# Two-layer graph convolution with scatter: final scatter moved last, dense work re-tiled in pairs of 1024 rows and spread over all stages

## The reference

```python
msg = x[src] @ W_msg + edge_attr @ W_edge
agg = segment_max(msg, dst)            # -inf -> 0 where a node has no edge
out = leaky_relu(agg + x @ W_root + b) # slope 0.01
```

## Time and profile before

| what | value |
|---|---|
| median of 3 runs | 1419.96 us (1419.81 to 1425.56) |
| profiled execution, span from first to last instruction | 1697.5 us (the page gives no other time of it) |
| DVE, POOL busy | 1044.2 us (62%), 1055.8 us (62%) |
| PE, ACT busy | 978.8 us (58%), 666.9 us (39%) |
| granted PE clock, mean | 0.746 |
| DMA | 245.87 MB, 145 GB/s over the span |

### The profile page before, as it was taken

The page is one execution under the profiler, slowest core; times in us unless marked ns, Lnnn a source line. Parts: engine busy times, 40 slices in busy tenths (PEclk is TensorE's granted clock), DMA queues, the critical chain, the costliest instruction groups (busy, mean ns, idle before and its releaser), DMA issues.

```text
span 1697.5 us, 21367 instructions
## 1 busy us (share of the span) xinstructions
PE 978.8 (58%) x3038; PEld 438.7 (26%) x3038; DVE 1044.2 (62%) x3881; ACT 666.9 (39%) x1717; POOL 1055.8 (62%) x1182
## 2 busy tenths in 40 slices
PE   3476866666666465687778778454343443334441
PEld 1233433233333232332322223222111111111210
DVE  2356666555555465679999999665544555445553
ACT  1345654444444354568888888400000000000000
POOL 5566656455545545617877767666667766677665
PEclk9678877778777777889999999755655655556555
DMA  6366756556555455755444444533333333233320
GB/s 172 93 183 207 240 178 181 174 175 194 175 177 184 146 179 171 220 177 185 157 153 154 152 146 154 164 111 106 104 95 94 107 99 104 79 102 99 107 74 21
DMA packets 142053, 245.87 MB, mean 145 GB/s; under 512 B 31470, under 2 KB 70120, under 8 KB 142022
## 3 DMA queue, kind: packets, MB, share of 16 engines
q1 hardware_dynamic: 103462, 161.26, 30.4%
q0 software_dynamic: 31360, 45.90, 11.5%
q10 hardware_dynamic: 7200, 38.40, 6.0%
HBM read 122.70 MB, written 125.07 MB: 146 GB/s over the span
## 4 chain that ended last, share of the span: by engine, by line
issue 34%; DVE 15%; PE 15%; another core or an unknown queue 15%; ACT 11%; POOL 4%; DMA 1%; DVEq 1%; ACTq 1%; POOLq 1%
ACT ob L686 5%; PE ps L529 5%; PE ps_r L529 4%; DVE stat L820 3%; PE ps_t L519 2%; POOL out L302 2%; PE ps_m L529 2%; DVE c1t L780 2%; DVE mv L831 2%; ACT c2t L647 2%; POOL g_src L295 2%; DVE c2t L780 2%; DVE stage L923 1%; DVE mx L790 1%
## 5 line engine op out<-in xcount | busy, mean ns | idle before, releaser
L686 ACT ACTIVATE ob<-ps_y,shift,rstd 128x96 f32<-128x96 f32 x784 | 273.7, 432 | 139.9 <-DVE shift L859 71.4
L820 DVE BATCH_NORM_STATS2 stat<-ps_y 128x6 f32<-128x96 f32 x784 | 147.0, 248 | 192.4 <-remote 141.1
L302 POOL DMA_INDIRECT agg_table<-stage,now_end x196 | 221.2, 1128 | 68.5 <-issue 68.2
L302 POOL DMA_INDIRECT out<-stage,now_end x196 | 200.4, 1022 | 60.0 <-issue 59.1
L295 POOL DMA_INDIRECT g_src<-in_x,now_gat x196 | 195.8, 999 | 63.0 <-issue 62.9
L295 POOL DMA_INDIRECT g_dst<-in_x,now_gat x196 | 195.2, 996 | 59.7 <-issue 59.1
L529 PE MATMUL ps<-xtb,wr 97*96 97x512 f32 x392 | 224.1, 655 | 11.0 <-ACT c1t L647 2.9
L295 POOL DMA_INDIRECT g_src<-agg_table,now_gat x196 | 196.8, 1004 | 52.9 <-issue 52.6
L529 PE MATMUL ps<-c1t,wr 97*96 97x512 f32 x392 | 212.4, 625 | 11.5 <-issue 10.3
L519 PE MATMUL ps_t<-ident,g_src 128*96 128x128 f32 x392 | 90.2, 374 | 209.9 <-DMA g_src<-agg_table,now_gat 176.7
L655 ACT ACTIVATE std<-mv,epsc 128x4 f32<-128x4 f32 x245 | 74.6, 305 | 296.5 <-issue 185.5
(11 more groups left out here) (54 smaller groups left out, 1494.3 us busy)
## 6 DMA issues: line engine op xcount, KB each, us to landing
xtb<-in_xt SPq DMA_DIRECT2D x196, 192.0 KB
agg_table<-zero ACTq DMA_DIRECT2D x50, 750.0 KB
out<-ob SPq DMA_DIRECT2D x195, 192.0 KB
mask<-mask_row SPq DMA_DIRECT2D x98, 192.0 KB
xd_keep<-g_dst SPq DMA_DIRECT2D x49, 192.0 KB
root_keep<-rt SPq DMA_DIRECT2D x49, 192.0 KB
c1d_keep<-c1d SPq DMA_DIRECT2D x49, 192.0 KB
rt<-root_keep SPq DMA_DIRECT2D x49, 192.0 KB
```

The source lines that it names most:

```text
L302: nc.gpsimd.indirect_dma_start(out=rows, out_offset=bass.IndirectOffsetOnAxis(ap=now_end[:, e.slot(R), r:r + 1], axis=0), in_=stage[:, e.s ...
L686: last = nc.scalar.activation(ob[:, d.slot(R), row(r)], ps_y[k][:, row(r)], ACT.Identity, bias=shift[:, k, r:r + 1], scale=rstd[:, k, r:r ...
L820: last = V.bn_stats(stat[:, k, r, :], rows(r))
```

## The change

All 49-chunk loops are written out (no hardware loops). POOL's program becomes four sequences. The number of indirect DMAs stays 980:

- A: 49 x 4 gathers of `x[src]`, and 7 chunks' gathers of `x[dst]` (28) among them.
- S: 49 x 4 table scatters, each chunk waiting only for the parts of the table that its rows fall in to be cleared (a number that POOL reads from a tile into a register). Then 3 chunks' gathers of `x[dst]` (12).
- B: 49 x 4 table gathers and 39 chunks' gathers of `x[dst]` (156).
- O: 49 x 4 scatters into `out`, each chunk waiting for the dense stores of its part of `out` only.

Index copies on POOL, the bounds check of the scatters and the tile `stage` go; DMAs read the index tiles directly and scatter from `nat`. Rows that must not be written go to spare rows behind the N rows. Each gather waits for the one three chunks before it to have landed (`FLIGHT = 3`). Each tile of the source gathers has its own semaphore.

Dense work is tiled in 98 **pairs** of 1024 rows: 14 beside stage A, 35 beside S, 25 in B and 24 behind them. `x` is loaded a second time in row order. The second product takes c1 as the stationary operand, so its result has rows on the partitions and the transposes back go. Leaky sums are made as relu(0.99 u) (ACT, from PSUM) plus 0.01 u + x (DVE, written to PSUM). `bn_stats` takes two rows at a time with an interleaved pattern and yields mean and sum without `bn_aggr`. Of the 8 rows per partition that are normalized, DVE takes 2 and ACT 6 (in stage B ACT takes 8).

The clears are 49 DMAs of 768 KB, 25 issued in A and 24 in S. c1 at `dst` is recomputed in B from `x[dst]` and `nat`, so `c1d_keep` and `xd_keep` go, and PE does more in B.

```diff
-ZCOL = 1500
-NZ = N * D // (P * ZCOL)
+J = 8
+RS = 6
+RD = 10
+NA = 14
+NS = 35
+NM = 25
+VROWS = 2
+AHEAD = 4
+LAND = 8
+FLIGHT = 3
+ZA = 25
...
+STEPS_A = spread(NA, NCH, 0)
+STEPS_S = spread(NS, NCH, NA)
+STEPS_B = spread(NM, NCH, NA + NS)
+STEPS_Z = spread(ZA, NCH, 0)
+SEAM = 3
+EARLY = {t: (t - 8) // 5 for t in range(8, 8 + 5 * (RD - SEAM), 5)}
...
+            for c in range(NCH):
+                gather_src(x, c, c)
+                if c in EARLY:
+                    pool.wait_ge(s_prep, 12)
+                    gather_dst(EARLY[c], c)
+
+            for c in range(NCH):
+                last = (c + 1) * TPC - 1
+                pool.wait_ge(s_zeroed, nc.gpsimd.value_load(zone_i[P - 1:P, last:last + 1], min_val=1, max_val=NZ))
+                pool.sem_inc(s_open, 1)
+                pool.wait_ge(s_open, c + 1)
+                scatter(table, c, sc_t, a_nc)
+            pool.wait_ge(s_zeroed, NZ)
+            for c in range(RD - SEAM, RD):
+                gather_dst(c, NCH)
+            for k in range(LAND):
+                pool.wait_ge(sc_t[k], 16 * ((NT + LAND - 1 - k) // LAND))
+
+            for c in range(NCH):
+                gather_src(table[0:N, :], c, NCH + c)
+                if RD <= c + AHEAD < NCH:
+                    gather_dst(c + AHEAD, NCH + c)
+
+            for c in range(NCH):
+                last = (c + 1) * TPC - 1
+                pool.wait_ge(s_stored, nc.gpsimd.value_load(pair_i[P - 1:P, last:last + 1], min_val=1, max_val=NQ))
+                pool.sem_inc(s_under, 1)
+                pool.wait_ge(s_under, c + 1)
+                scatter(out, c, sc_o, e_done)
...
+                for j in range(HJ):
+                    last = nc.tensor.matmul(ps_z[:, h, row(j)], c1t[:, q % 2, cols(h * HJ + j)], wr2[:, :],
+                                            start=True, stop=True)
...
+                for r in range(TPC):
+                    nc.tensor.matmul(ps_n[:, row(r)], c1d[:, c % 2, cols(r)], wr2[:, :], start=True, stop=False)
+                    last = nc.tensor.matmul(ps_n[:, row(r)], mx2[:, c % 2, cols(r)], ident[0:D, 0:D],
+                                            start=False, stop=True)
...
+                    nc.tensor.matmul(ps_r[0:D, :], wr1[0:D, :], xd[:, c % 2, :], start=True, stop=False)
+                    for r in range(TPC):
+                        last = nc.tensor.matmul(ps_r[0:D, cols(r)], nat[:, c * TPC + r, :], ident[:, :],
+                                                start=False, stop=r == TPC - 1)
...
+                t = ps_z[:, h, 0:HJ * D]
+                V.scalar_tensor_tensor(out=t, in0=t, scalar=SLOPE, in1=xn[:, k, halfrow(h)],
+                                       op0=ALU.mult, op1=ALU.add).then_inc(d_u, 1)
...
+                for j in range(0, J, 2):
+                    last = V.bn_stats(stat[:, q % 2, j:j + 2, :].rearrange("p r s -> p (r s)"),
+                                      two_rows(yo[:, q % YR, j * D:(j + 2) * D]))
...
+                for j in range(on_vector(q)):
+                    t = yo[:, q % YR, row(j)]
+                    last = V.tensor_scalar(t, t, stat[:, q % 2, j, 1:2], rstd[:, q % 2, j:j + 1],
+                                           ALU.subtract, ALU.mult)
```

More of the change, by code:

```diff
@@ L46, with spread, gnn_kernel @@
 SLOPE = 0.01
-ZCOL = 1500
-NZ = N * D // (P * ZCOL)
[L49 to L113, removed]
+ZROWS = 2048
+ZCOL = ZROWS * D // P
+NZ = -(-N // ZROWS)
+ZTAIL = (N - (NZ - 1) * ZROWS) * D // P
+ZR = 4
+NA = 14
[6 more added lines that the diff above has]
+ZA = 25
+assert NZ == NCH and NQ == 2 * NCH and (N - (NQ - 1) * PN) % J == 0
+def spread(count, ticks, first):
+    return {t: range(first + t * count // ticks, first + (t + 1) * count // ticks) for t in range(ticks)}
+STEPS_A = spread(NA, NCH, 0)
+STEPS_S = spread(NS, NCH, NA)
+STEPS_B = spread(NM, NCH, NA + NS)
+LATE = NA + NS + NM
+STEPS_B[NCH] = range(LATE, LATE + 1)
+STEPS_B[NCH + 1] = range(LATE + 1, LATE + 2)
+STEPS_Z = spread(ZA, NCH, 0)
+STEPS_Y = {t: range(ZA + t, ZA + t + 1) for t in range(NZ - ZA)}
+SEAM = 3
+EARLY = {t: (t - 8) // 5 for t in range(8, 8 + 5 * (RD - SEAM), 5)}
+def gnn_kernel(nc, x, xt, src, dst, dst_next, dst_row, dst_prev, aside, eat,
                w1m, w1e, w1r, b1, w2m, w2e, w2r, b2, out):
@@ L637, in _ @@
+            for d in range(LATE + 1, NQ + 1):
+                for h in range(2):
+                    dense(range(d, d + 1), h)
         @block.scalar
@@ L728, in _ @@
-            clear(NZ - 1)
-            each_chunk(act, step_a)
-            maxima(LAST_CHUNK)
-            def step_s(q, s, last=False):
-                c = chunk(q, s)
-                act.wait_ge(a_nc, c.at + 1)
-                if c.reached(2):
-                    act.wait_ge(sc[c.slot(2)], 64 * c.turn(2))
-                copy(stage[:, c.slot(2), :], nat[:, ds(c.at * TPC * D, TPC * D)], s_stage)
-                for t in range(2):
-                    dense(block_s(q, s, t))
-            each_chunk(act, step_s)
@@ new lines, in dense_norm, with dense_head @@
+            def dense_norm(q):
+                if not real(q):
+                    return
+                act.wait_ge(d_shift, q + 1)
+                for j in range(on_vector(q), J):
+                    last = nc.scalar.activation(yo[:, q % YR, row(j)], yo[:, q % YR, row(j)], ACT.Identity,
+                                                bias=shift[:, q % 2, j:j + 1], scale=rstd[:, q % 2, j:j + 1])
+                last.then_inc(d_done_a, 1)
+            def dense_head(steps):
+                for d in steps:
+                    dense_std(d - 2)
+                    dense_r(d - 1, 0)
+                    dense_t1(d, 0)
@@ L758, in _ @@
+            for d in range(LATE + 2, NQ + 2):
+                dense_head(range(d, d + 1))
+                dense_tail(range(d, d + 1))
         @block.vector
```

1146 lines of the change are left out of this document (560 added, 586 removed).

## The result

The changed kernel takes **1245.9 us** (median of 4 runs, 1245.5 to 1246.9) against 1419.9 us for the kernel before on the same chip: a ratio of 0.878, interval 0.875 to 0.881. The profiled execution spans 1244.1 us, so here, unlike before, the profile shows what the runs do.

A forecast was written before the change was run, and what follows sets the result against it. POOL's issue pace, 1.0 us plus a 0.3 us gap per indirect DMA, was taken as the bound. Terms 5 + 285 + 282 + 18 + 470 + 253 + 15 + 7 = 1335, rounded to 1332 us; range 1195 to 1415.

The forecast's parts named there:

- the forecast's own case: Whole kernel: POOL's pace sets the time, 1290 to 1375 us; chance 0.54.
- cheap POOL: Rival, whole kernel: POOL is cheaper in the runs than in the profile, 1215 or 1190 us; chance 0.17.
- POOL's floor: Kernel before: POOL's own time without the stalls of A and B, 1358 us, 62 us below the median run.
- The register loads: Stages S and O: 49 loads each at 0.3 us, 15 us a stage; bounds 0 to 147 us together.
- two chains of equal length that meet cost more than either; I take 9.6: Stage B: POOL and the engines' loop both need 9.0 us a chunk, taken as 9.6, so 470 us.
- The cover: Stage O: the 24 last pairs take 137 us on DVE and stay ahead of POOL's scatters by 50 us or more.
- B with PE's clock above 0.9: Sign for stage B: PE's clock above 0.9, at 9 to 10 us a chunk.
- The SBUF rule: Stages A, S, O: two-port DVE operations lock POOL's descriptor writes, at most 50 us; by the profile row, nothing.
- S as DVE's stage: Old stage S: DVE busy 299.75 of 309 us sets the pace, and POOL waits for it, 6.1 us a tick.
- The longer stage B: Rival, stage B: dense and edge work wait for each other, 10.5 to 11.3 us a chunk, 1375 to 1415; chance 0.15.
- dear register loads: Rival, POOL's register loads: 1.5 us each as POOL cannot read ahead, 117 us more, 1450 us; chance 0.05.
- The slower case: Rival, stage B: waits keep PE's clock at 0.6, B takes 710 us and the kernel 1570; chance 0.09.

The follow-up runs named there:

- 4 runs: The changed kernel, unaltered, timed four times against the kernel before on the same chip: median 1245.9 us against 1419.9, ratio 0.878.

## Why the prediction was right, and where its steps were off

The forecast was 1332 us, the range 1195 to 1415; it came out at 1246. The direction and its ground, POOL's issue pace, held. The size did not: the gain is 174 us where 88 were forecast, and 1246 lies below the forecast's own case (1290 to 1375). The range holds it only because it reached down to 1195 for a rival, cheap POOL, that did not come. That part is luck. By the steps:

| step | predicted us | measured us |
|---|---|---|
| start | 5 | 3 |
| A | 285 | 280 |
| S | 282 | 248 |
| own gathers, drain | 18 | 15 |
| B | 470 | 441 |
| O, register loads, last landing | 275 | 257 |
| sum | 1335 | 1244 |

- **What bounds the kernel: right.** To take POOL's floor in place of the profiled span's stalls was the choice on which all rested. The loops written out show the old kernel at that pace, and in the changed one POOL has no other wait at all.
- **A: right** within 5 us. The allowance for gathers that have not landed was not needed at 241 GB/s and a DMA share of 0.80.
- **S: 34 us too long**, from three terms. The register loads (15) cost nothing: the gap ahead of a chunk's first scatter is 0.30 to 0.31 us as ahead of the others. The long scatters (12) are gone. The pace was 1.264 us and not 1.3 (7). ("21 of 49 parts are cleared" should read 25; nothing hung on it.)
- **B: 29 us too long.** POOL's own 440 us were right to the microsecond. What failed is the step "two chains of equal length that meet cost more than either; I take 9.6". The engines' pace is 8.5 us and not 9.0, and the own gathers run 4 chunks ahead; this slack, as I read it, took up the swing between chunks with and without a pair, and POOL loses nothing. The loop's own working does not add up either: 7.5 + 1.9 + 2.8 is 12.2 and not 10.5 us with a pair, unless the two additions overlap, which I had not said.
- **O:** 248 and 9 us for 253, 15 and 7; the register loads again. The cover was thinner than I wrote. I counted from POOL's end of B (987 us), while PE ends its edge work 39 us later. The last pair is normalized at 1195 and POOL needs the last at about 1230: some 30 us are left, and five more pairs would have shown.
- **PE's clock: wrong.** "B with PE's clock above 0.9" measured 0.85, with no cost. "At half clock PE would be busy all the time" is what did happen, but in S and O: 240 of 245 us busy at 0.53, a pair at 6.7 us where I had 4.1. 35 pairs of 6.7 us fill S, and PE ends them 34 us after POOL has left S. So S is now nearly PE's too: with 1.3 us more a pair, in the run with transposes, POOL began to wait. The Trainium skill ("TensorE: Matmul & The Clock Gate", Part 1) has the clock follow how busy PE has been, by which it should be full there. The rows disagree: 0.50 at 225 of 229 us busy.
- **The SBUF rule: weighed on the wrong side.** I asked whether the new DVE operations would lengthen POOL's DMAs, found no sign beside `stage<-yn`, and took nothing for them, which came out: 0.5 us in all beside L802, against the 50 us at most "by the rule". The row that I went by was a weak witness, though: L923 takes 0.34 us and could lengthen a DMA by little. But I never asked it of the operations that the change *removes*. The earlier trace rows held a scatter of 1.46 us, and I called it one in four without looking at what DVE did at its start. This is the largest single part of the difference between the two POOL streams, some 75 of 162 us, and it is in no term of the sum; the durations that I took, 1.0 + 0.3, were an average that had it in.
- **S as DVE's stage: only half.** "DVE is full and POOL waits for it" does not stand: the tick of 6.1 us has no wait of POOL in it. It is 1.46 + 3 x 0.98 for scatters, 0.19 for the copy, and gaps of 0.57 ahead of the first scatter, 3 x 0.30 and 0.04. DVE was full, and POOL was held by it inside its DMAs. In S 31 us of the lengthening lie; whether POOL would have had to wait for DVE instead, without it, no run tells.
- **Rivals.** The cheap-POOL case was nearer in time (1215), not in kind: the gaps stay 0.30 us, and no overlap was bought by shorter ones. The longer stage B and the dear register loads did not come. The slower case came in a form that I had not priced: not PE's clock, but a chip on which engines stall. There the ratio is 1.024.
- **"A profile of the changed kernel should be slower than its runs"** failed: 1244.1 and 1245.9. I took the gap of 277 us for something that profiling adds to this kernel. The profile with the loops written out, 1406.3 us beside 1408.0, has no such gap. By its span the execution that I read looks like one on a slower chip; on which it ran is not on record.

The runs on the single parts also show what these are: not gains over the old order, but what the new one depends on. Moving the dense pairs out of B, or waiting for all clears, gives back 122 of the 174 us each; waiting for all stores gives back more than all of it.

## What to carry to other kernels

An engine at 76% busy can be the bound: here POOL was. Count its instructions and the fixed gap ahead of each; where the two fill the span, only fewer or shorter instructions help, and everything else needs only to stay beneath. Ask of a long DMA issued by POOL what DVE ran at its start: sums with both inputs in SBUF were running at the start of 315 of 980 here and cost them 0.24 us each; beside the changed kernel's sums with an operand in PSUM (L766) 81 DMAs were not longer at all. Where profile and runs differ by 20%, take the span as a sample of another condition, and ask of a plan with little slack between engines what it does when they stall.

## What the runs showed of the hardware that was not expected

- PE's granted clock is 0.50, its 1.2 GHz level, while its records are busy 100.00 of 100 us with the fp32 products of the new pairs alone, and 0.99 in the old S at 79%. Transposes in S and a silent POOL in O did not change it; edge chunks between the pairs go with a clock of 1.00 (565 to 600 us).
- A DMA that POOL issues while DVE runs a wide operation with two inputs from SBUF is longer by what is left of that operation less 0.12 us (75 of 75 isolated cases within 0.03 us with the loops written out, 14 of 14 in the changed kernel). Scans and sums that read PSUM did nothing to it.
- A wait of POOL on a value loaded from a tile into a register costs nothing beside its DMAs (98 times, gaps of 0.30 to 0.31 us).
- An indirect DMA on POOL takes 0.944 us (gather) or 0.958 (scatter) as a median; what the memory moved beside them made no difference: the scatters' mean is 0.958 us from 300 to 400 us in the changed kernel, at 390 GB/s, and 0.961 in O of the run that waited for all stores, at 39 GB/s. The bounds check adds 0.015 to 0.02.
- One kernel on one core differs by 18 to 22% between chips, with stalls of ACT, DVE and PE that have no releaser in the trace; the changed kernel differs by 42%.
